# Node layers 0 and 1: another order of the words in the exchanged x

## The reference, cut to what matters

```
x = layernorm(x + relu(concat([x, segment_max(x[dst] - x[src], dst)]) @ W0 + b0))   # layer 0
x = layernorm(x + L1(x, edge_attr_54, edge_attr_18, edges))                          # layer 1
# inside L1, for nodes without an edge: x = swish(x @ lin.T + lin_b); two swish branches,
# a product with cat, three residual swish layers, then a norm over all nodes
```

## Time and profile before

| | |
|---|---|
| median of 3 runs | 5658.59 us |
| lowest, highest | 5655.28, 5660.55 us |
| span of the profiled execution, first to last instruction | 5689.4 us |
| mean granted TensorE clock | 0.862 |
| PE busy | 4597.0 us, 81% of the span |
| PE weight loads busy | 2788.2 us, 49% |
| DVE busy | 4328.5 us, 76% |
| ACT busy | 3650.3 us, 64% |
| POOL busy | 4126.8 us, 73% |
| HBM traffic | 648.60 MB read, 438.76 MB written |

### The profile page before, as it was taken

One profiled execution on the slowest core, in us unless ns is written; L12 is line 12 of the kernel. 1 busy time (PEld: TensorE's weight loads), 2 busy tenths in 40 slices (PEclk: granted clock), 3 DMA queues, 4 the chain that ended last, 5 costly groups with the idle time before them and its releaser, 6 DMA issues. The chain is left out here.

```text
span 5689.4 us, 82998 instructions
## 1 busy us (share of the span) xinstructions
PE 4597.0 (81%) x18558; PEld 2788.2 (49%) x18558; DVE 4328.5 (76%) x8746; ACT 3650.3 (64%) x9127; POOL 4126.8 (73%) x4125
## 2 busy tenths in 40 slices
PE   6999999999999997899999999999777656662000
PEld 4555555555555543344444467777555434441000
DVE  7777777777777765688888789999788864447776
ACT  3666666666666663566666668888688863336665
POOL 5777777777777767677777357777777767777777
PEclk9999999999999998999999999999855556665555
DMA  5666666666666654677777689999888866665443
GB/s 163 183 186 179 177 181 186 186 176 179 182 186 181 176 153 121 204 203 207 203 207 203 186 296 363 363 365 366 294 286 283 281 212 223 220 218 173 138 134 105
DMA packets 699928, 1213.28 MB, mean 213 GB/s; under 512 B 146894, under 2 KB 366472, under 8 KB 699686
## 3 DMA queue, kind: packets, MB, share of 16 engines
q1 hardware_dynamic: 594038, 1059.81, 59.1%
q0 software_dynamic: 100352, 149.23, 10.2%
q10 hardware_dynamic: 5296, 1.73, 0.1%
HBM read 648.60 MB, written 438.76 MB: 191 GB/s over the span
## 5 line engine op out<-in xcount | busy, mean ns | idle before, releaser
L839 ACT ACTIVATE p_s<-p_ps,cols 128x512 f32<-128x512 f32 x588 | 403.9, 687 | 597.1 <-PE p_ps L793 400.9
L716 POOL DMA_INDIRECT p_xs<-in_x,src_cols x388 | 424.9, 1095 | 271.7 <-DVE p_r L898 182.4
L723 POOL DMA_INDIRECT home<-edge_row_cols,scatter_cols x392 | 442.9, 1130 | 119.3 <-issue 119.0
L191 POOL DMA_INDIRECT u_rows<-t_rows,home_cols x392 | 406.9, 1038 | 145.5 <-issue 118.2
L198 POOL DMA_INDIRECT out<-u_res,scatter_cols x392 | 407.7, 1040 | 121.8 <-issue 118.4
L1188 POOL DMA_INDIRECT ring_rows<-t_rows,home_cols x384 | 408.5, 1064 | 119.3 <-issue 88.6
L191 POOL DMA_INDIRECT ring_rows<-t_rows,home_cols x400 | 399.1, 998 | 126.3 <-issue 117.1
L716 POOL DMA_INDIRECT p_xd<-in_x,dst_cols x388 | 397.3, 1024 | 107.5 <-issue 97.1
L1197 POOL DMA_INDIRECT home_cols<-home,src_cols x376 | 368.6, 980 | 145.1 <-issue 86.0
L787 PEld LDWEIGHTS p_ps<-w_swapped,p_xT 128*128 128x128 f32 x1568 | 400.1, 331 | 121.3 <-issue 82.0
L787 PE MATMUL p_ps<-w_swapped,p_xT 128*128 128x128 f32 x1568 | 389.2, 393 | 39.2 <-DMA p_xT<-p_xt 32.1
(11 more groups left out here) (304 smaller groups left out, 14037.8 us busy)
## 6 DMA issues: line engine op xcount, KB each, us to landing
ring_rows<-in_x SPq DMA_DIRECT2D x98, 512.0 KB, 5.8
p_xT<-p_xt SPq DMA_DIRECT2D x392, 128.0 KB
t_rows<-p_o SPq DMA_DIRECT2D x98, 512.0 KB
p_x1T<-p_oT SPq DMA_DIRECT2D x392, 128.0 KB
hT<-ring_own SPq DMA_DIRECT2D x98, 512.0 KB
q_hn<-hT SPq DMA_DIRECT2D x98, 512.0 KB, 4.0
r_h<-hT SPq DMA_DIRECT2D x98, 512.0 KB
r_x<-t_rows SPq DMA_DIRECT2D x98, 512.0 KB
```

The source lines that it names most:

```text
L191: nc.gpsimd.indirect_dma_start(out=rows[:, j, :], out_offset=None, in_=table, in_offset=bass.IndirectOffsetOnAxis(ap=idx[:, j:j + 1], axis ...
L716: nc.gpsimd.indirect_dma_start(out=rows[:, j, :], out_offset=None, in_=a["x"], in_offset=bass.IndirectOffsetOnAxis(ap=idx[:, j:j + 1], axi ...
L723: nc.gpsimd.indirect_dma_start(out=tab["home"], out_offset=bass.IndirectOffsetOnAxis(ap=s["scat"][:, k:k + 1], axis=0), in_=s["at"][:, k:k ...
L839: nc.scalar.activation(act_out[i][:, :], flat(bank_r), ACT.Silu, bias=col(LS0 + i)).then_inc(r_act[i], 1)
```

## The change: what it does

The two tiles of the exchange get another order of their free dimensions. In p_xt, for each buffer and each column group c, the words stood as 32 rows i, then 2 blocks, then 4 slots j; now 2 blocks, 4 slots, then 32 rows. In p_xT they stood as 4 partition groups a, 32 rows, 2 blocks, 4 slots; now 2 blocks, 4 slots, 4 partition groups, 32 rows. So a stationary operand of line 787, one slot of one block, was 128 words with a step of 8 words, and is 128 words in a row. The output of the turn was written with a step of 8 words and is written in runs of 32 words. Each of the four DMAs of the exchange moved 128 runs of 1,024 bytes; on the side that it writes it now has 8 runs of 128 bytes for each partition, 1,024 runs in all, 128 KB as before. The products, their operands' values and every semaphore stay.

```diff
-        x_turned, xT = sb("p_xt", [P, 2, 4, 32, 2, G]), sb("p_xT", [P, 2, 4, 32, 2, G])
+        x_turned, xT = sb("p_xt", [P, 2, 4, 2, G, 32]), sb("p_xT", [P, 2, 2, G, 4, 32])
...
-                    swap_groups(sp, xT[:, q % 2], x_turned[:, q % 2], xT_in[q % 2])
+                    swap_groups(sp, xT[:, q % 2].rearrange("p h j a i -> p a (h j) i"), x_turned[:, q % 2], xT_in[q % 2])
...
-                        i = nc.tensor.matmul(bank_o[:, j, :], xT[:, q.of(2), :, :, t.slot % 2, j].rearrange("p a i -> p (a i)"), first["w0"][:, :],
+                        i = nc.tensor.matmul(bank_o[:, j, :], xT[:, q.of(2), t.slot % 2, j].rearrange("p a i -> p (a i)"), first["w0"][:, :],
                                              start=True, stop=True)
...
-                turn_squares(nc, x_turned[:, q.of(2), :, :, n.slot % 2, :].rearrange("p c i j -> p c j i"),
-                             x[:, n.of(8)]).then_inc(x_squared, 1)
+                turn_squares(nc, x_turned[:, q.of(2), :, n.slot % 2], x[:, n.of(8)]).then_inc(x_squared, 1)
```

## The result

The changed kernel takes 5727.59 us (median of 4 runs, 5724.29 to 5742.14) against 5659.57 (4 runs, 5655.28 to 5668.46): 68 us slower, a ratio of 1.0123 with a 95% interval of 1.0107 to 1.0138. The forecast was 5741, 82 us slower, with a range of 5630 to 5860. Ratios of all kernels here are formed from fast executions; one of the four of runs_256_first took 10,563.85 us at a mean granted clock of 0.455 and is in its median but not in its ratio.

What follows compares the result with a forecast made beforehand. TensorE was taken as the bound at 21.0 us a pair; after the change the loop through the landing, 19.6 + 2.2 = 21.8 us, adds 0.84 us a pair, 82 in all: 5658.6 + 82 = 5741 us, range 5630 to 5860.

Steps and rivals of the forecast that it cites:

- The bound passes from TensorE to the landing: The pair is set by the landing of p_xT, 21.8 us, no longer by TensorE's work, 18.6 us after the change.
- The sum: Loop over scan, SP's queue and landing: 19.6 us plus 2.2 for the exchange, 21.8 against 21.0: 82 us slower in all.
- The exchange: 2.2 us: Exchange of p_xT in 128-byte runs takes 3.7 us of every DMA engine instead of 1.5; all 2.2 us delay the landing.
- the low bound: Only the last of the exchange's four DMAs counts, so the landing comes 0.55 us later.
- The weight loads: 1.18 us in each step: Line 787's eight loads go from 0.259 to 0.111 us each: 1.18 us less a step, 2.36 a pair.
- From the turn to the end of the scan: 6.0 us,: Behind the landing: about 1.3 us to line 934, then 4.68 us to the end of the scan.
- The issues: SP's four issues of the exchange of p_xT take 2.52 us as before; more runs do not lengthen an issue.
- In nearly every pair: Line 787 and the turn wait for p_xT in nearly every pair, with about 3 us of PE idle each.
- The clock granted in full: TensorE's clock stays granted in full in this stage; a fall would make the kernel slower yet.
- The first, that the landing stays in time: Exchange costs under 1.4 us more, so the pair shortens and the kernel is faster: 5580 or 5525, floor 5425; chance 0.17.
- The doubled price below 512 bytes: Read-modify-write doubles the exchange's 3.7 us: landing 5.9 us later, 6100 us; part of a rival with chance 0.13.
- The rival that the weight loads would not get quicker: Line 787's loads stay at 0.259 us despite words in a row: loop 23.0 us, kernel 5855 us; chance 0.05.

Runs made afterwards that it cites:

- runs_256_first: Kernel before with 256-byte runs, operand and turn at a step of 2 words, exchange of p_xT at the head of SP's turn: 5496.59 us, ratio 0.9703.
- short_first: Kernel before with 128-byte runs only (operand and turn at a step of 8 words), exchange of p_xT at the head of SP's turn: 5640.72 us, ratio 0.9955.
- after_first: Changed kernel with the exchange of p_xT moved to the head of SP's turn, ahead of the wait for the scan: 5482.08 us, ratio 0.9686.
- before_first: Kernel before the change with its exchange of p_xT (1,024-byte runs) moved to the head of SP's turn: 5639.73 us, ratio 0.9956.
- after_mid: Changed kernel with the exchange of p_xT put ahead of that of p_x1T, both still behind the scan: 5577.01 us, ratio 0.9847.

## Why the prediction was right, point by point

**The bound passes from TensorE to the landing.** Right, and shown from both sides: with the exchange out of the loop the same operand and the same runs give 0.9686, and the short runs alone change nothing (0.9955 against 0.9956, 20.69 us for a pair in both).

**The sum.** 0.84 us for a pair were forecast, and 0.58 measured (0.66 by the estimate above). Three terms were mis-sized, and they leaned against each other: in the pairs in which the turn waits the three stretches were 6.7 + 8.8 + 6.3 = 21.8 us, the forecast's own sum, where it had 6.45 + 9.4 + 6.0. That the sum comes out to the tenth is luck; the direction is not.

- **The exchange: 2.2 us.** In the pair shown it is 8.81 - 7.21 = 1.6 us from the first issue to the turn, 1.36 in the means, and the short runs alone cost 1.54 us in a pair. It lies between my value and the low bound. The runs' own time had not been overrated: in the pair shown 4,182 of them pass in 4.25 us on 16 engines, 16.3 ns each, so 256 take 4.2 us where I had 3.7. What was wrong is that all of it would show; why some of it does not was not tried apart. The busy share is no better guide. At the same GB/s it went from 0.67 to 0.83 (short_first), 0.16 x 20.7 = 3.3 us of each engine in a pair. But after_first against before_first gives 0.85 x 18.89 - 0.67 x 20.69 = 2.2 us, and the changed kernel against the one before 0.71 x 21.58 - 0.67 x 21.00 = 1.3. The exchange's packets are the same in all three comparisons, so the share must hold stalls as well.
- **The weight loads: 1.18 us in each step.** I counted from the second load of lines 804 and 805 on and so left out the gap after the first. With it, line 787 goes from its first load at 1029.56 to the next line's at 1030.77 us, 1.21 us against 2.07: 0.86 less. At the head of SP's turn, where TensorE sets the pace, before_first and after_first differ by 20.69 - 18.89 = 1.80 us for a pair, 0.90 for a step. TensorE's floor is 18.9 us and not 18.6. It is also part of the next point: with the clock in full, line 933 started 1031.08 - 1029.56 = 1.5 us after the first load, where I had 1.3.
- **From the turn to the end of the scan: 6.0 us,** as 1.3 + 4.68. In the pair shown it is 1048.88 - 1042.17 = 6.7, and 6.3 in the means. Of the 0.7 us in this pair 0.6 come before line 933: 0.1 before the first load, 0.2 are the point above, and 0.3 I put down to TensorE's clock, below.

**The issues.** Wrong. That "the number of runs does not seem to lengthen an issue" rested on one store of 784 runs that met an empty queue, and on my own count of one DMA where four come in a row. It took 2.48 us for the third. It is inside the landing's time, so the sum did not suffer twice.

**In nearly every pair.** Not quite: the turn waits in 55 pairs of 65, and PE in 48. Behind a pair with a long wait the next often needs none: pairs in which nothing waits take 19.9 to 20.6 us, those with a wait of over 2.5 us on VectorE mostly 22 to 23.8. So the 21.8 us of the waiting pairs become 21.58 on average. The mean wait of PE is 105.5 / 65 = 1.6 us for a pair, half of what I wrote.

**The clock granted in full.** Wrong, on a term that I had put at nothing. In the changed kernel, the window right behind the wait:

```profile
1042.20:1046.00 3.80, 3.73 (x13) 2.60 (x14) 3.11 (x7) 0.32 (x1) 2.89 (x4) 0.57 0.43 159
```

PE had been idle for 2.3 us ahead of it, and went on at 0.57, nearly the lower of its two levels (1.2 GHz); the two passes of line 793 took 1.91 us where they took 1.02. Over the stage it is 0.96. The prediction had named this as a thing that would make it slower yet. In the pair shown line 933 starts 1044.06 - 1042.27 = 1.79 us after the first load, against 1.52 at full clock: 0.3 us of the loop, an estimate from one pair. Next to 0.58 that is not small. How much of the 0.58 us it is was not tried apart. The four kernels without the wait have a clock of 1.00 in the stage, but so has after_mid, with waits of up to 3.0 us on PE: not every wait brings the clock down.

**The rivals.** The first, that the landing stays in time, had its threshold at 1.4 us; the measured 1.4 to 1.6 is at it or just past it, which was nearer than a chance of 0.17 says. With 256 bytes the kernel is faster, 0.9954, though the landing does not stay in time there: it costs less than the words with a step of 2 give. The doubled price below 512 bytes fell: at 128 bytes the landing moved by 1.4 to 1.6 us and not by 5.9. What the Trainium skill says in DMA: Bandwidth & Descriptors, section Why small descriptors are slow (HBM only), that copies inside SBUF are spared the penalty, is nearer to that, but free they are not: with the same bytes the DMA share rose from 0.67 to 0.83. The rival that the weight loads would not get quicker was wrong for steps of 1 and 2 words, and would have been right for 4.

## What to carry to other kernels

Where a transfer lands just in time at the end of a loop through a DMA queue, its price is the wait it makes, and its place in the queue can be worth more than its shape: the same short runs cost 2.9% at the end of the queue's turn and nothing at its head. Before shortening an engine's work, look which transfer is next in line to be late, move that away first, and only then take the gain; here the change and the move together give 0.9686, while alone they give 1.0123 and 0.9956. And try the sizes between: half of a layout change can bring all of its gain, as a step of 2 words did here.

## What the runs showed of the hardware

- A float32 stationary operand of 128 columns with a step of 2 words loads in 199 ns on average, one with a step of 1 in 200 (some of these at a lower clock; medians in the kernels with the exchange at the head are 196 and 192), with 4 in 325, with 8 in 331. VectorE's transpose of 32x32 squares writes with a step of 1 in 689 ns, with 2 in 688, with 4 in 1,089, with 8 in 1,085. The edge lies between a step of 8 bytes and one of 16; from 16 to 32 nothing changes.
- Four DMAs issued in a row by SP with 64 runs for each engine took 4.74 us on average in place of 2.52, and the third took 2.48 in the pair shown; with 32 runs some were long, up to 2.94 us; with 16 none, at most 0.67. That fits a queue with room for some 130 runs for each engine, two DMAs of 64 or four of 32. It is an estimate from these rows, and no run tried the room apart.
- The exchange in 256 runs of 128 bytes for each engine kept the DMA engines busy for 1.3 to 3.3 us in a pair more than the same bytes in 32 runs of 1,024, in three comparisons of kernels, where the line through the rows had 2.2. In one burst they passed at 16.3 ns a run on each engine, where it had 14.4. The busy share is not a price that can be carried from one of these kernels to another.
